# Rotary attention in quadrants: changed tile shapes and orders on four engines

## What is computed

```
xq = rope((x @ Wq).reshape(b, s, 16, 8))
xk = rope((x @ Wk).reshape(b, s, 4, 8))
xv = (x @ Wv).reshape(b, s, 4, 8)
keys, values = repeat(xk, 4), repeat(xv, 4)
scores = einsum('bqhd,bkhd->bhqk', xq, keys) / sqrt(8)
scores = where(abs(q - k) <= 16, scores, -inf)
ctx = einsum('bhqk,bkhd->bqhd', softmax(scores), values)
return ctx.reshape(b, s, 128) @ Wo
```

## Time and profile before

| | us |
|---|---|
| median of 3 executions | 3638.08 (3636.49 to 3638.13) |
| profiled execution, its own time | 3631.84 |
| its span on the core | 3629.9 |
| rotary attention, weight load to last add | 87.6 to 304.2, some 217 |
| granted TensorE clock, mean of the span | 0.933 of full |

### The profile page before, as it was taken

The page is one execution under the profiler, slowest core; times in us unless marked ns, Lnnn a source line. Parts: engine busy times, 40 slices in busy tenths (PEclk is TensorE's granted clock), DMA queues, the critical chain, the costliest instruction groups (busy, mean ns, idle before and its releaser), DMA issues. The chain is left out here.

```text
span 3629.9 us, 108450 instructions
## 1 busy us (share of the span) xinstructions
PE 3268.1 (90%) x40814; PEld 2730.2 (75%) x40816; DVE 2528.6 (70%) x7254; ACT 1815.8 (50%) x4530; POOL 1241.1 (34%) x1823
## 2 busy tenths in 40 slices
PE   5887899999989999897899999999999999774866
PEld 4776899999967777545788998898999898643345
DVE  6784899999968888657455655555655555478765
ACT  3331787877757777574433333333333333224463
POOL 4562888888833333303300000000000000155032
PEclk8996999999999999898799999999999999877677
DMA  4001000000022222200365554555555555264000
GB/s 122 1 0 38 1 0 0 0 0 0 1 64 79 78 78 79 57 1 7 87 129 132 132 130 122 139 128 133 131 131 123 138 127 133 67 113 71 0 3 26
DMA packets 375492, 254.10 MB, mean 70 GB/s; under 512 B 118676, under 2 KB 371560, under 8 KB 374536
## 3 DMA queue, kind: packets, MB, share of 16 engines
q1 hardware_dynamic: 370824, 245.44, 28.0%
q10 hardware_dynamic: 4352, 4.20, 0.5%
HBM read 233.53 MB, written 15.75 MB: 69 GB/s over the span
## 5 line engine op out<-in xcount | busy, mean ns | idle before, releaser
L2462 PE MATMUL psum<-L_xattn_ctxT,L_xattn_q_ctx 128*128 128x257 f32 x2048 | 511.2, 390 | 2.1 <-DMA L_xattn_ctx<-ctx_dram 2.1
L1061 PE MATMUL psum<-L_ffn_share,L_ffn_prob 128*128 128x128 f32 x4096 | 487.9, 278 | 23.2 <-DVE L_ffn_prob L994 15.2
L878 POOL TENSOR_TENSOR L_ffn_sums<-L_ffn_sims 128x1024 f32<-128x1024 f32 x256 | 485.0, 1911 | 61.4 <-DVE L_ffn_prob L994 61.4
L2493 PEld LDWEIGHTS psum<-L_xattn_probT,L_xattn_ctx 32*128 32x128 f32 x16384 | 468.9, 187 | 44.6 <-issue 42.0
L1061 PEld LDWEIGHTS psum<-L_ffn_share,L_ffn_prob 128*128 128x128 f32 x4096 | 471.3, 193 | 35.9 <-DVE L_ffn_prob L994 25.7
L2493 PE MATMUL psum<-L_xattn_probT,L_xattn_ctx 32*128 32x128 f32 x16384 | 493.2, 273 | 2.1 <-DVE L_xattn_probT L2376 2.1
L2314 ACT ACTIVATE L_xattn_prob<-psum,L_xattn_nmax 128x258 f32<-128x258 f32 x512 | 238.8, 471 | 478.7 <-DVE L_xattn_nmax L2362 462.0
L2285 POOL TENSOR_TENSOR L_xattn_z_var<-L_xattn_z_mv,L_xattn_z_eps 128x1 f32<-128x1 f32 x32 | 6.1, 190 | 1248.4 <-DVE L_xattn_z_mv L2388 1219.1
L2462 PEld LDWEIGHTS psum<-L_xattn_ctxT,L_xattn_q_ctx 128*128 128x128 f32 x2048 | 369.0, 191 | 64.3 <-issue 5.5
L920 ACT ACTIVATE psum<-L_ffn_sums,L_ffn_bias 128x512 f32<-128x512 f32 x512 | 339.1, 686 | 63.6 <-DVE L_ffn_prob L994 58.7
L994 DVE SCALAR_TENSOR_TENSOR L_ffn_prob<-L_ffn_sums,L_ffn_best,psum 128x512 f32<-128x512 f32 x512 | 358.4, 742 | 6.9 <-ACT psum L920 3.8
(11 more groups left out here) (459 smaller groups left out, 6567.2 us busy)
## 6 DMA issues: line engine op xcount, KB each, us to landing
L_xattn_ctx<-ctx_dram SPq DMA_DIRECT2D x512, 256.0 KB, 3.9
L_xattn_ctxT<-ctx_T_dram SPq DMA_DIRECT2D x128, 257.0 KB, 3.2
L_xattn_k_all<-ctx_T_dram SPq DMA_DIRECT2D x128, 128.5 KB, 2.1
L_xattn_v_all<-ctx_dram SPq DMA_DIRECT2D x128, 128.0 KB, 2.2
L_attn_qkv_scratch<-L_attn_qkv SPq DMA_DIRECT2D x24, 256.0 KB, 2.8
L_attn_rows<-L_attn_qkv_scratch SPq DMA_DIRECT2D x24, 256.0 KB, 5.3
start_raw<-ctx_dram ACTq DMA_DIRECT2D x16, 256.0 KB, 11.8
L_xattn_v_rows<-L_xattn_v SPq DMA_DIRECT2D x8, 256.0 KB, 2.3
```

Source lines behind the costliest of these rows:

```text
L878: nc.gpsimd.tensor_tensor(sums[:, h % RING, :, :], sx, sy, ALU.add).then_inc(summed, 1)
L1061: last = nc.tensor.matmul(pair(2 * s)[:, c * P:(c + 1) * P], prob[:, h % RING, c * P:(c + 1) * P], share[:, h % RING, :], start=(h == 0 an ...
L2462: last = nc.tensor.matmul(scores(s)[:, g, 0:CTX], q_ctx[:, p, c, b, h:h + 4, :].rearrange("p h n -> p (h n)"), ctxT[:, b, c, :], start=(c ...
L2493: last = nc.tensor.matmul(mix_bank(r)[:, c * P:(c + 1) * P], ctx[rows, b, k, c * P:(c + 1) * P], probT[rows, b % 2, k, :, :].rearrange("p ...
```

## The change

VectorE's step starts with the rotation and adds the output after it. The normalisation of tile t+1 leaves VectorE: ScalarE does it as an activation with a scale and a bias of each row, and GpSimd makes the bias (`shifted_mean`, minus mean times reciprocal deviation) in one further instruction. GpSimd makes these factors ahead of the shares. ScalarE copies the values last in its step. The mix of sequence b writes PSUM partitions 32b to 32b+31, so that its copy is 128 partitions by 128 columns in place of 32 by 512. The output becomes 16 products of 32 by 32 stationary elements, sequence b with rows and output partitions 32b on; for this `w_o` is loaded four times, into four groups of partitions. TensorE's steps are all written out, with no loop.

```diff
--- before.py
+++ after.py
@@ -582,7 +582,7 @@
         w_qk = sb("w_qk", [D, 4, D])
 
         w_v = sb("w_v", [D, G, G * 8])
-        w_o = sb("w_o", [G * 8, G, D])
+        w_o = sb("w_o", [P, G, D])
         qk = sb("qk", [P, W, 2, P])
         prod = sb("prod", [P, W, 2, P])
         q4 = sb("q4", [P, W, BT, G, SEQ])
@@ -591,20 +591,21 @@
         prob = sb("prob", [P, W, HEADS, SEQ])
         top = sb("top", [P, W, HEADS])
         total = sb("total", [P, W, HEADS])
+        shifted_mean = sb("shifted_mean", [P, W])
         probT = sb("probT", [P, W, BT, P])
-        mixT = sb("mixT", [G * 8, W, G, P])
+        mixT = sb("mixT", [P, W, G, SEQ])
         bank_a = lambda s: core.psum[:, 2 * s, :]
         bank_b = lambda s: core.psum[:, 2 * s + 1, :]
         front = Front(core, st, name, W, bank_a)
         (w_in, zeroed, projected, v_done, roped, masked, scored, shifted, exped, summed, normal, turned, probT_done,
-         mixed, mixT_done, out_done, added) = (core.sem(f"{name}_{n}") for n in (
+         mixed, mixT_done, out_done, added, centred) = (core.sem(f"{name}_{n}") for n in (
              "w_in", "zeroed", "projected", "v_done", "roped", "masked", "scored", "shifted", "exped", "summed",
-             "normal", "turned", "probT_done", "mixed", "mixT_done", "out_done", "added"))
+             "normal", "turned", "probT_done", "mixed", "mixT_done", "out_done", "added", "centred"))
         block = st.enter_context(nc.Block())
 
         @block.sync
         def _(sp):
-            load(sp, [(w_qk[:, :, :], dram[f"{name}_Wqk"]), (w_o[:, :, :], dram[f"{name}_Wo"])], w_in)
+            load(sp, [(w_qk[:, :, :], dram[f"{name}_Wqk"]), *((w_o[32 * b:32 * b + 32, :, :], dram[f"{name}_Wo"]) for b in range(BT))], w_in)
             sp.wait_ge(zeroed, 1)
             load(sp, [(w_v[:, g, 8 * g:8 * g + 8], dram[f"{name}_Wv"][:, 8 * g:8 * g + 8]) for g in range(G)], w_in)
 
@@ -617,16 +618,22 @@
                 a, m = spread(qk[:, s, 1, :].rearrange("p (b w) -> p b w", b=BT), core.c("group"), SEQ)
                 nc.gpsimd.tensor_tensor(kbd[:, s, :, :, :], a, m, ALU.mult).then_inc(masked, 1)
 
+            def normal_factors(t, s):
+                front.pool_rstd(pool, t - s, only=s)
+                pool.drain()
+                nc.gpsimd.tensor_scalar(shifted_mean[:, s:s + 1], front.mv[:, s, 0:1], front.rstd[:, s, :], -1.0, ALU.mult,
+                                        ALU.mult).then_inc(centred, 1)
+
             def normalise(t, s):
                 pool.wait_ge(summed, t + 1)
                 nc.gpsimd.tensor_tensor(prob[:, s, :, :], prob[:, s, :, :], per_row(total[:, s, :]),
                                         ALU.mult).then_inc(normal, 1)
 
             def step(t, j, live):
+                if live(-1):
+                    normal_factors(t + 1, (j + 1) % W)
                 if live(3):
                     normalise(t - 3, (j - 3) % W)
-                if live(-1):
-                    front.pool_rstd(pool, t + 1 - (j + 1) % W, only=(j + 1) % W)
                 if live(1):
                     mask(t - 1, (j - 1) % W)
 
@@ -639,6 +646,11 @@
                 act.wait_ge(turned, t + 1)
                 nc.scalar.copy(probT[:, s, :, :], bank_a(s).rearrange("p (b w) -> p b w", b=BT)).then_inc(probT_done, 1)
 
+            def normalise(t, s):
+                act.wait_ge(centred, t + 1)
+                nc.scalar.activation(front.xn[:, s, :], core.x[:, ds(t, 1), :].rearrange("p a d -> p (a d)"), ACT.Identity,
+                                     bias=shifted_mean[:, s:s + 1], scale=front.rstd[:, s, :]).then_inc(front.normed, 1)
+
             def exp(t, s):
                 act.wait_ge(shifted, t + 1)
                 nc.scalar.activation(prob[:, s, :, :], prob[:, s, :, :], ACT.Exp).then_inc(exped, 1)
@@ -649,20 +661,21 @@
 
             def mix_copy(t, s):
                 act.wait_ge(mixed, t + 1)
-                nc.scalar.copy(mixT[:, s, :, :].rearrange("p h (b q) -> p b h q", b=BT),
-                               bank_b(s)[0:G * 8, :].rearrange("p (b h q) -> p b h q", b=BT, h=G)).then_inc(mixT_done, 1)
+                nc.scalar.copy(mixT[:, s, :, :], bank_b(s)[:, 0:P].rearrange("p (h q) -> p h q", h=G)).then_inc(mixT_done, 1)
 
             def step(t, j, live):
                 if live(0):
                     front.act_copy(act, t - j, only=j)
                 if live(3):
                     turn_copy(t - 3, (j - 3) % W)
-                if live(0):
-                    v_copy(t, j)
+                if live(-1):
+                    normalise(t + 1, (j + 1) % W)
                 if live(2):
                     exp(t - 2, (j - 2) % W)
                 if live(3):
                     mix_copy(t - 3, (j - 3) % W)
+                if live(0):
+                    v_copy(t, j)
 
             pipelined(act, W, -1, 4, step)
 
@@ -697,13 +710,13 @@
 
             def step(t, j, live):
                 o, q = (j - 1) % W, (j - 2) % W
-                if live(4):
-                    dve.wait_ge(out_done, t - 3)
-                    add_to_x(core, t - 4, bank_a(j)[:, 0:D]).then_inc(added, 1)
                 if live(1):
                     turn_pairs(t - 1, o)
                     dve.drain()
                     join_pairs(o)
+                if live(4):
+                    dve.wait_ge(out_done, t - 3)
+                    add_to_x(core, t - 4, bank_a(j)[:, 0:D]).then_inc(added, 1)
                 if live(2):
                     raw = bank_b(q).rearrange("p (a w) -> p a w", w=SEQ)
                     add_band(t - 2, q)
@@ -715,8 +728,6 @@
                     front.dve_moments(dve, t + 2 - (j + 2) % W, only=(j + 2) % W)
                 if live(2):
                     sums(t - 2, q)
-                if live(-1):
-                    front.dve_normalise(dve, t + 1 - (j + 1) % W, only=(j + 1) % W)
 
             front.dve_moments(dve, 0, only=0)
             pipelined(dve, W, -1, 4, step)
@@ -751,14 +762,17 @@
                 pe.wait_ge(v_done, t + 1)
                 pe.wait_ge(probT_done, t + 1)
                 for b in range(BT):
-                    last = nc.tensor.matmul(bank_b(s)[0:G * 8, b * P:(b + 1) * P], vbd[:, s, b, :], probT[:, s, b, :],
+                    last = nc.tensor.matmul(bank_b(s)[32 * b:32 * b + 32, 0:P], vbd[:, s, b, :], probT[:, s, b, :],
                                             start=True, stop=True)
                 last.then_inc(mixed, 1)
 
             def out(t, s):
                 pe.wait_ge(mixT_done, t + 1)
                 for h in range(G):
-                    last = nc.tensor.matmul(bank_a(s)[:, 0:D], mixT[:, s, h, :], w_o[:, h, :], start=(h == 0), stop=(h == G - 1))
+                    for b in range(BT):
+                        own = slice(32 * b, 32 * b + 32)
+                        last = nc.tensor.matmul(bank_a(s)[own, 0:D], mixT[own, s, h, :], w_o[own, h, :], start=(h == 0),
+                                                stop=(h == G - 1))
                 last.then_inc(out_done, 1)
 
             def step(t, j, live):
@@ -777,8 +791,9 @@
                 if live(3):
                     out(t - 3, (j - 3) % W)
 
-            pe.wait_ge(w_in, 16 * (2 + G))
-            pipelined(pe, W, -1, 4, step)
+            pe.wait_ge(w_in, 16 * (1 + BT + G))
+            for t in range(TILES + 4):
+                step(t, t % W, lambda lag: 0 <= t - lag < TILES)
 
 
 def product_key_experts(core, name):
```

## The result

Measured together, the kernel before has a median of 3637.28 us (3633.38 to 3638.13, 4 runs) and the changed one 3601.32 us (3595.71 to 3603.85, 4 runs): a ratio of 0.9898, interval 0.9882 to 0.9914. The forecast was 3611, with a range of 3603 to 3628. The profiled execution took 3595.71. In the table, the times of the columns before and after are read in the two profiled executions.

What follows compares the result with a forecast made beforehand. The prediction took a closed ring of waits, 6.08 us a tile, to bound the stage, falling to 5.25. Terms -23.8, -4.4 and +1.4 gave -26.8 on 3631.84, so 3605.0, plus 6.2 to the median: 3611, range 3603 to 3628.

Steps and rivals of the forecast that it cites:

- The old ring: Before the change, add, rotation, masks, scores and output product wait on each other in a closed ring of 6.08 us a tile.
- its two successors: Next rings per tile: VectorE's own work without waiting, 5.22 us, and TensorE's way through the add, 5.26; taken as 5.25.
- Mix and output: TensorE's products in quadrants: mix 0.39 us to the next product, output 1.10 us for 32 overlapping passes.
- The rival without overlap: The output's quadrants, all writing one bank, do not overlap: output 3.7 us, whole time 3705 us; chance 7%.
- The edits at nothing: GpSimd's extra instruction and factors, ScalarE's normalisation, the mix's copy in the loop and the values' copy last, costed at nothing.
- the cover of 0.6: Masks end 3.4 us after the rotation starts, TensorE reaches the scores at 4.0, leaving 0.6 us.
- The start: Stage start: three more copies of w_o ahead of TensorE's last weight DMA lose 1.4 us, or nought if transfers overlap.
- The end: Last three tiles, 20.95 us at 1.2 GHz: shorter mix and copy gain 4.4 us, leaving 16.5.
- The sum: Whole execution: -23.8 for 28 tiles, -4.4 at the end, +1.4 at the start, giving -26.8 us.
- the steady part: The 28 tiles between first and 29th add: 170.79 us before, 147.0 after, a gain of 23.8.
- How the numbers follow: The prediction's step that weighed its cases, forecast 67%, and set the range of 3603 to 3628 us.
- periods of 5.5 to 5.9: Rival of a smaller gain: rings disturb each other or the exponential is delayed, 3616 to 3630 us; chance 18%.

Runs made afterwards that it cites:

- e3: The kernel before with only VectorE's rotation put ahead of its add; median 3627.03 us, ratio 0.9981, tile 5.83 us.
- e4: The changed kernel with mix, its copy, output and the load of w_o as before, TensorE still written out; 3615.82 us, ratio 0.9954, tile 5.75 us.
- e5: The kernel before with mix, copy and output in quadrants and TensorE written out, orders and normalisation as before; 3629.49 us, ratio 0.9975, tile 5.97 us.
- e10: The changed kernel with VectorE's loop written out too; 3605.17 us, ratio 0.9916, tile still 5.19 us.
- e6: The changed kernel with the same 32 output passes written quadrant by quadrant; 3652.77 us, ratio 1.0043, tile 6.47 us.
- e7: The changed kernel with GpSimd's factors put back behind the share; 3607.55 us, ratio 0.9916, tiles 5.47 us on average.
- e8: The changed kernel with the normalisation back on VectorE and GpSimd's shifted mean dropped; 3612.11 us, ratio 0.9933, tile 5.38 us.
- e1_null: The kernel before with only a comment added, also called the null; 3633.62 us, ratio 1.0002.

## Why the prediction was right, and where not

- **The old ring, and its two successors: right.** The wait for the output is gone, the masks no longer hold the scores, and 5.24 on average stands against 5.25. e3, e4 and e5 show that the parts have to come together. Of the two bounds only VectorE's binds, 5.19 against 5.22. The prediction read those 5.22 as time in which VectorE runs without waiting; that is wrong, though the size is right. The sums stood 0.03 behind the exponential before too, with 1.39 from the subtraction, and e10 shows that this part does not shorten when VectorE's work in it does. As for TensorE's bound: it came to 4.99, not 5.26: add to transpose 0.34 for 0.42, scores to output 1.09 for 1.15, output to add 0.06 for 0.16, and 0.03 in mix and output.
- **Mix and output: right,** 0.38 and 1.08 for 0.39 and 1.10. The rival without overlap is out: even e6's order, the worse of the two tried, overlaps in part and costs 3653, not 3705. The Trainium skill, TensorEngine Tiling (Array Packing), section Gotcha 1: PSUM Pressure, says that different row tiles cannot access the same bank at once. The trace does not agree for this case: four row tiles whose column tiles differ too write one bank, and their passes start 7 ns apart, 32 of them in 1.08 us.
- **The edits at nothing: right in their places,** but not free. ScalarE's copy of the values, put last at no price, keeps the exponential from waiting for it; by e3's rows the old place would hold the tile at some 5.56 (an estimate, not run). e7 shows that the factors' place is not free to choose: the cover of 0.6 for the masks is 0.36. e8 shows that the normalisation's 0.19 is a real term of VectorE's ring.
- **"The start" was off in its net size.** Net 0.34 lost, 1.1 better than forecast: TensorE's first product came 0.86 later and not 1.4, and from there to the first add it was 0.52 shorter. Why is not shown, and e1_null, with the code of before, takes 25.20 in place of 24.59, so 0.6 of it can be scatter.
- **"The end" failed: the step that set three tiles at 1.2 GHz on both sides.** It took one execution's late clock as the stage's own. In that execution the clock fell within 1 us of the 29th add; it fell 10 us after it in the null and some 8 us after it in the two profiles of the changed kernel, once for good and once only in passing. e1_null, with the same code as before, needs 17.81 for the last three tiles, the changed kernel 13.63 and 14.71. Forecast 4.4 gained, measured 7.32; against the null it is 3.1 to 4.2, so the size of 4.4 would have been about right for two executions with a like clock.
- **The sum.** 26.8 forecast, 30.9 in the stage: 2.9 from the end, 1.1 from the start, 0.2 from the steady part. With these 4.1 alone the median would have been 3606 to 3607, inside the range. The rest of the span, 5.1 shorter in the profile and put at nothing in the sum, took it out; 0.8 more is the median of before, 3637.28 with a fourth execution in place of 3638.08.
- **The range failed at "How the numbers follow".** Its low end, 3603, held only bounds of the terms, none for the scatter of the 3413 us that the change does not touch, which alone moves by up to 17.7 from profile to profile, nor for the end's clock. A median 5 us to either side belonged inside it. Another slip there changed nothing: periods of 5.5 to 5.9 less 5.25 are 0.25 to 0.65 a tile, 3618 to 3629, not 0.18 to 0.58.

## What to carry to other kernels

Follow the wait back until the ring closes, and then work out the next ring and the one after it before pricing an edit: here the halves of the change alone took 0.11 and 0.33 us off the tile, and only together 0.89. A ring can also hide beside another of the same length: the way through the exponential took as long as VectorE's own work between subtraction and sums, and showed only when that work shrank. Order decides inside a ring: on GpSimd the same instructions in another order cost 6 us, and on VectorE a rotation moved into an apparent hole lengthened the tile by 0.19. What is worth nothing in one place may be needed there, like the values' copy behind the exponential. Size a stage's end from more than one execution if the clock changes in it, and give a range room for what the untouched stages scatter.

## What was not expected of the hardware

- Passes of different row and column tiles overlap on one bank: 32 in 1.08 us when they alternate, and still 2.46 when eight of one tile come in a row, since the next tile's passes begin 0.467 after.
- The granted clock of the stage's end differs between executions of the same code: it fell within 1 us of the 29th add in the profile before and 10 us after it in the null. During the 28 tiles the change held 1.00, while e6, with the same products in another order, was granted 0.93, with eight short falls. What brings them on was not tried.
- Between the mix, with 32 columns of weights (L765), and the scores, with 128, the weight load shows about 0.2 us in which it waits for nothing in the profile, 28 times:

```profile
PEld psum L750 <- issue: 5.6, 28, 0.2
```
